# Attention scores in rounded and rest parts, two reordered item pipelines' starts, and a graph-attention shift built from one-column operations, in a one-core four-block kernel

## The reference, cut to what matters

```python
qkv = nodes @ Wqkv.T + bqkv                                    # attention, block 1
q = q.reshape(n, H, DH) * DH ** (-0.5)
scores = jnp.einsum('nhd,mhd->hnm', q, k)
probs = jax.nn.softmax(scores, axis=-1)
attn = jnp.einsum('hnm,mhd->nhd', probs, v).reshape(n, D)
...
gates = jax.nn.softmax(x @ Wg + bg, axis=-1)                   # experts, block 2
topg, topi = jax.lax.top_k(gates, 2)
h = jax.nn.gelu(jnp.einsum('bnc,ech->ebnh', x, W1) + b1, approximate=False)
y = jnp.einsum('ebnh,ehc->bnec', h, W2) + b2
...
e = jax.nn.leaky_relu(a_src[src] + a_dst[dst], NEG_SLOPE)      # graph attention, block 3
m = jax.ops.segment_max(e, dst, num_segments=n)
ex = jnp.exp(e - m[dst])
```

## Time and profile before

| | |
|---|---|
| median of 3 runs | 1318.64 us (1318.53 to 1323.35) |
| the profiled execution's own time | 1322.17 us |
| its span | 1320.1 us |
| busy: PE, PEld, DVE, ACT, POOL | 95%, 84%, 71%, 45%, 8% |
| attention heads | about 500 to 625 us |
| first expert block's items | about 665 to 1003 us |
| graph attention, first layer's heads | about 1079 to 1151 us |

### The profile page before, as it was taken

One profiled execution on the slowest core, in us unless ns is written; L12 is line 12 of the kernel. 1 busy time (PEld: TensorE's weight loads), 2 busy tenths in 40 slices (PEclk: granted clock), 3 DMA queues, 4 the chain that ended last, 5 costly groups with the idle time before them and its releaser, 6 DMA issues. The chain is left out here.

```text
span 1320.1 us, 19406 instructions
## 1 busy us (share of the span) xinstructions
PE 1251.7 (95%) x7067; PEld 1111.7 (84%) x7068; DVE 942.5 (71%) x1771; ACT 598.0 (45%) x1044; POOL 107.0 (8%) x111
## 2 busy tenths in 40 slices
PE   5999999999999999999999999999999888899997
PEld 4777569999999996776999999999998778896864
DVE  6577665583583476668879999999998788736624
ACT  4111143341441245346438888898885227412210
POOL 0000100000000000000030000000002018500111
PEclk9999999999999999999899999999999999999899
DMA  9531190420420610024366999999998210008135
GB/s 348 168 95 33 46 361 24 156 72 1 156 72 1 239 51 0 1 73 155 144 251 242 377 391 392 392 389 394 382 399 278 92 29 1 1 1 298 48 109 166
DMA packets 80704, 225.47 MB, mean 171 GB/s; under 512 B 5185, under 2 KB 17025, under 8 KB 80513
## 3 DMA queue, kind: packets, MB, share of 16 engines
q1 hardware_dynamic: 72736, 187.64, 38.4%
q0 software_dynamic: 7904, 36.97, 7.8%
HBM read 197.85 MB, written 26.74 MB: 170 GB/s over the span
## 5 line engine op out<-in xcount | busy, mean ns | idle before, releaser
L2297 DVE TENSOR_TENSOR part_slot<-slot,item_hi 128x768 fp32r<-128x768 f32 x156 | 138.7, 954 | 1.9 <-ACT item_hi L1673 1.5
L1673 ACT ACTIVATE item_hi<-slot 128x768 fp32r<-128x768 f32 x156 | 118.1, 833 | 30.6 <-DMA slot<-in_e0w 24.8
L2306 DVE TENSOR_TENSOR part_slot<-slot,item_hi 128x768 fp32r<-128x768 f32 x132 | 116.6, 953 | 0.6 <-ACT item_hi L1681 0.2
L1681 ACT ACTIVATE item_hi<-slot 128x768 fp32r<-128x768 f32 x132 | 99.2, 832 | 10.3 <-DMA slot<-in_e0w 10.3
L756 PE MATMUL dve_ps<-item_hi,x_hi 128*128 128x384 f32 x288 | 99.3, 345 | 1.3 <-DVE part_slot L2297 1.0
L756 PE MATMUL act_ps<-item_hi,hid_hi 128*128 128x384 f32 x288 | 99.1, 344 | 0.3 <-DVE hid_lo L2500 0.3
L757 PE MATMUL act_ps<-part_slot,hid_hi 128*128 128x384 f32 x288 | 97.4, 338 | 0.0
L758 PE MATMUL dve_ps<-item_hi,x_lo 128*128 128x384 f32 x288 | 97.2, 338 | 0.0
L758 PE MATMUL act_ps<-item_hi,hid_lo 128*128 128x384 f32 x288 | 96.7, 336 | 0.0
L757 PE MATMUL dve_ps<-part_slot,x_hi 128*128 128x384 f32 x288 | 95.7, 332 | 0.0
L1537 ACT ACTIVATE h_t<-act_ps,par 128x256 f32<-128x256 f32 x36 | 21.1, 585 | 106.9 <-PE act_ps L880 106.9
(11 more groups left out here) (442 smaller groups left out, 3308.2 us busy)
## 6 DMA issues: line engine op xcount, KB each, us to landing
slot<-in_e0w SPq DMA_DIRECT2D x48, 2304.0 KB, 10.5
slot<-in_w SPq DMA_DIRECT2D x9, 2304.0 KB, 8.7
experts<-in_e1w SPq DMA_DIRECT2D x8, 1152.0 KB, 15.7
ea_raw<-in_edge SPq DMA_DIRECT2D x8, 1024.0 KB, 5.6
slot<-in_wqkv SPq DMA_DIRECT2D x3, 2304.0 KB, 15.3
xs<-zrow POOLq DMA_DIRECT2D x2, 3072.0 KB, 15.7
item_x<-xs SPq DMA_DIRECT2D x16, 384.0 KB, 9.5
ys<-item_y POOLq DMA_DIRECT2D x16, 384.0 KB, 6.5
```

Of the source, the lines that this page charges most:

```text
L1673: go(item_hi[j][k][:, :], slot[s][:, k * D:(k + 1) * D], ACT.Copy).then_inc(up_high[j], 1)
L1681: go(item_hi[j][k][:, :], slot[s][:, k * D:(k + 1) * D], ACT.Copy).then_inc(down_high[j], 1)
L2297: vv.tensor_tensor(part_slot[s][:, ks], slot[s][:, ks], item_hi[j][k][:, :].bitcast(F32), ALU.subtract).then_inc(up_low[j], 1)
L2306: vv.tensor_tensor(part_slot[s][:, ks], slot[s][:, ks], item_hi[j][k][:, :].bitcast(F32), ALU.subtract).then_inc(down_low[j], 1)
```

## The change

- The query and the key are split like the other operands. ScalarE rounds the query (`high_query`: two Copies, after VectorE's `query`), and `key` now writes rounded parts. VectorE makes the rests (`low_query`: two subtractions; `low_key`: two `scalar_tensor_tensor` from the bank). The half of the key that the next scores need is made first and has a signal of its own; the bank is freed by the second half's rest. Scores are `mm_parts`.
- The first item's iteration is written out in another order: the down product comes before the next item's up product, its weights are rounded and subtracted while the first up product runs, and SP loads the second item's down weights before the third item's up weights. Some dummy matmuls go.
- In `graph_front` the two 128x4 operations become eight of 128x1 with one SBUF tile input each and a per-partition scalar (one after each masking step, four at the end).
- The load of `slot_iota` is issued later, as its place now holds the query's rounded part before.

```diff
 def scores(i):
-    pe.wait_ge(sig.dve_freed, v0 + HEAD_UNIT[f"q{made_of(i)}"] + 1)
-    pe.wait_ge(sig.act_freed, a0 + HEAD_UNIT[f"k{made_of(i)}"] + 1)
+    pe.wait_ge(qv_low, parted(f"q{made_of(i)}"))
+    if i == made_first(made_of(i)):
+        pe.wait_ge(qv_low, parted(f"k{made_of(i)}"))
+    else:
+        pe.wait_ge(sig.act_freed, a0 + HEAD_UNIT[f"k{made_of(i)}"] + 1)
...
-        mm(bank[:, :], query_of(i)[:, t * P:(t + 1) * P], key_of(i), start=True, stop=True
-           ).then_inc(sig.to_act, 1)
+        mm_parts(bank[:, :], (high[:, ts], low[:, ts]), key_of(i), start=True, stop=True).then_inc(sig.to_act, 1)
...
 # ScalarE
+def high_query(b):
+    act.wait_ge(sig.dve_freed, DVE0["heads"] + HEAD_UNIT[f"q{b}"] + 1)
+    chunk, hd = chunk_of(b)
+    go(q_hi[:, b % 2, :], q_t[:, b % 2, :], ACT.Copy)
+    go(q_split_hi[chunk, hd, :], q_split[chunk, hd, :], ACT.Copy).then_inc(qkv_high, 1)
...
                 for name in BETWEEN[i].split():      # after the exponentials, before prb_hi
                     if name[0] == "k":
                         key(int(name[1]))
+                    else:
+                        high_query(int(name[1]))
 # VectorE
                 divide(i)
...
+                for name in BETWEEN[i].split():      # after low_out, where slot 5 has it; before prb_lo
+                    if name[0] == "k":
+                        low_key(int(name[1]))
+                    else:
+                        query(int(name[1]))
+                        if f"q{made_of(i + 1)}" == name:
+                            low_query(int(name[1]))
...
                 if i + 1 < NH:
                     maxima(i + 1)
+                    for name in BETWEEN[i].split():
+                        if name[0] == "q" and f"q{made_of(i + 1)}" != name:
+                            low_query(int(name[1]))
 # TensorE, items
-iteration(0)
+turn_hidden(0)
+spend(up_banks[0][0], 6)
+pe.wait_ge(x_low, 4)
+for j, s in enumerate(run.down_slots):
+    times_down(0, j, s, down_low, 0)
+times_up(1)
+turn_x(2)
 with pe.Fori(1, last) as k:
 # ScalarE, items
 keep_rows(run, 0); x_in(0)
+high_down(0, 0)
 keep_rows(run, 1)
+high_down(1, 0)
 x_in(1)
-iteration(0, True)
-with act.Fori(1, last) as k:
+gelus(0)
+high_up(0, 1, down_used, 0)
+high_up(1, 1, down_used, 0)
+x_in(2)
+iteration(1, True)       # high_up(0, 2), gelus(1), high_up(1, 2), high_down(0), high_down(1), ...
+with act.Fori(2, last) as k:
 # VectorE, items
-for j in range(2):
-    hidden(0, j)
+hidden(0, 0); low_down(0, 0); hidden(0, 1)
 x_in(1)
+low_hidden(0); low_down(1, 0); low_up(0, 1); result(0); low_up(1, 1)
 share_last(run)
-iteration(0, True)
+hidden(1, 0); hidden(1, 1); x_in(2)
+iteration(1, True)
 # VectorE, graph attention
+    if t:
+        then(raise_max(t - 1))       # tensor_scalar(gdec[..., t], gmax[..., t], a_dst[:, t], 0.0, add, max)
...
-vv.scalar_tensor_tensor(gdec[:, b, 1, :], gmax[:, b, :], -5.0, part_dst[:, 1, :, g % GH], ALU.mult, ALU.subtract)
-vv.scalar_tensor_tensor(gdec[:, b, 2, :], gmax[:, b, :], -1.0, gdec[:, b, 1, :], ALU.mult, ALU.min).then_inc(g_dec, 1)
+raise_max(NT - 1).then_inc(sig.dve_freed, 1)
+for t in range(NT):
+    last = vv.tensor_scalar(gdec[:, b, 2, t:t + 1], gdec[:, b, 1, t:t + 1], -4.0, gmax[:, b, t:t + 1], ALU.mult, ALU.subtract)
```

More of the change, by code:

```diff
@@ L74 @@
 BETWEEN = ("q1 k1", "q2 k2", "q3", "k3 q4", "k4 q5", "k5", "", "")
+HIGH_ORDER, LOW_ORDER = ["v0", "q0", "k0", "k0 second"], ["q0", "k0", "v0"]
+for _i in range(NH):
+    _late = ["v1"] if _i == 0 else []
+    for _name in BETWEEN[_i].split():
+        HIGH_ORDER += [_name] if _name[0] == "q" else [_name, _name + " second"]
+    HIGH_ORDER += _late
+    LOW_ORDER += BETWEEN[_i].split() + _late
 HEAD_UNIT = {"q0": 0, "k0": 0, "score0": 1}
@@ L491, in made_of, with made_first, whole_first, rounded @@
             return hd if hd < WHOLE else 3 * (hd - WHOLE) + 2
+        def made_first(b):
+            return next(i for i in range(NH) if made_of(i) == b)
+        def whole_first(b):
+            return HEADS[made_first(b)] < WHOLE
         def query_of(i):
             hd = HEADS[i]
-            return q_t[:, hd % 2, :] if hd < WHOLE else q_split[:, hd - WHOLE, :]
+            return (q_hi[:, hd % 2, :], q_lo[:, hd % 2, :]) if hd < WHOLE else (
+                q_split_hi[:, hd - WHOLE, :], q_split_lo[:, hd - WHOLE, :])
         def key_of(i):
             hd = HEADS[i]
-            return k_t[:, hd % 2, :] if hd < WHOLE else k_split[:, hd - WHOLE, :]
+            return (k_hi[:, :], k_lo[:, :]) if hd < WHOLE else (k_split_hi[:, hd - WHOLE, :], k_split_lo[hd - WHOLE][:, :])
+        def rounded(name):
+            return HIGH_ORDER.index(name) + 1
+        def parted(name):
+            return LOW_ORDER.index(name) + 1
         def chunk_of(b):
@@ L611, in _ @@
                 up_of(run0, 0, j)
+            sp.wait_ge(sig.to_act, ACT0["heads"] + HEAD_UNIT[f"score{NH - 1}"] + NT)
+            sp.dma_start(slot_iota[:, :], iota_d[0:P].partition_broadcast(P)).then_inc(in_tri, 16)
             sp.wait_ge(sig.to_dve, DVE0["wo"] + 8)
@@ L634, in stream_items @@
                 load_x(2)
-                with sp.Fori(1, last) as i:
+                for j, s in enumerate(run.down_slots):
+                    sp.wait_ge(down_used[j], DC)
+                    down_of(run, first, j, s)
+                second = expert(2)
+                for j in range(2):
+                    sp.wait_ge(up_used[j], 2 * DC)
+                    up_of(run, second, j)
+                sp.wait_ge(x_turned, 6)
+                load_x(3)
+                with sp.Fori(2, last) as i:
                     next_up = expert(i + 1)
@@ L1634, in high_attn @@
                 go(attn_hi[:, k, :], attn_t[:, k, :], ACT.Copy).then_inc(attn_high, 1)
+            high_query(0)
             key(0)
@@ L2239, in _ @@
             query(0)
+            low_query(0)
+            low_key(0)
             maxima(0)
@@ L2533, in stream_items @@
                 low_up(1, 0)
-                for j in range(2):
-                    hidden(0, j)
+                hidden(0, 0)
+                low_down(0, 0)
+                hidden(0, 1)
                 x_in(1)
-                share_last(run)
-                iteration(0, True)
-                with dve.Fori(1, last) as k:
+                low_hidden(0)
+                low_down(1, 0)
+                low_up(0, 1)
+                result(0)
+                low_up(1, 1)
+                share_last(run)
+                hidden(1, 0)
+                hidden(1, 1)
+                x_in(2)
+                iteration(1, True)
+                with dve.Fori(2, last) as k:
                     iteration(k)
```

98 lines of the change are left out of this document (65 added, 33 removed).

## The result

The changed kernel takes 1329.94 us (median of 13 runs, 1325.14 to 1333.39) against 1319.04 for the one before (1313.73 to 1326.89): a ratio of 1.0062 [1.0044, 1.0080], 8.2 us slower by that ratio, which is what everything below is measured against (the two medians alone stand 10.9 apart; the runs of the kernel before spread over 13 us). The profiled execution has a span of 1327.4 us, 7.3 more. The prediction said 1316.8. The time lies above its range, on the other side of no change.

A forecast was written before the change was run, and what follows sets the result against it. It took TensorE to bound the attention, TensorE and VectorE the item stream, VectorE the graph attention. Graph attention -3.9, attention +2.6 and items -0.6 sum to -1.9, on the median 1318.64 about 1316.8 us, range 1312 to 1321.

The forecast's parts named there:

- the first head's "0": Attention, first head: query and key split with nothing before them, +0.7 on the start, -0.7 in the matmuls: 0.
- the start of the third item's up product: Items' start: after the third item's rows are turned at 711.8, its up product starts at 715.2.
- the late rounding: Attention, three slots: ScalarE's queue holds high_query ahead of the probabilities' rounding; scores end +0.93 us later per slot, +2.8.
- the one-column operations: Graph attention: 128x1 operations run beside GpSimd without a stall, 0.07 us each; about 0.75 gained per stalled head.
- The graph attention, -3.9: Graph attention: sum of gains from replacing VectorE's stalled 128x4 operations, -3.9 us, bounds -0.7 and -4.3.
- GpSimd's and ScalarE's loop of 7.2: Graph attention: their own loop per head, about 7.2 us, against 7.1 for the new VectorE loop.
- Rival B: Graph attention: one-column operations take the lock and wait for GpSimd steps, +13 to +25, total 1334 to 1345; chance 0.10.
- The attention, +2.6: Attention: late roundings +2.8, other slots -0.4, slot 5 +0.5, last head -0.35; sum +2.6 us, bounds -5.2 and +4.5.
- The items, -0.6: Items' start: gains of 1.0 and 0.65 against 1.0 lost to the clock; sum -0.6 us, bounds -6 and +2.
- 0.65 more because weights come earlier: Items' start: a gain of 0.65 us from earlier weights, an item taking 27.12 instead of 27.77.
- my term of +1.0: Items' start: TensorE's new idle stretches without dummy matmuls lower the clock, a loss of 0 to 1.7, taken as 1.0.
- Rival C: Whole kernel: splits cost more and stalls cut the clock; attention +4.5, items +2, graph attention -2, total 1323; chance 0.13.

The follow-up runs named there:

- the parts alone: The kernel before with only the attention's, only the items' or only the graph attention's edits, three kernels: +5.9, +2.9 and -2.8 us.
- graph_only: The kernel before with the graph attention's one-column operations alone: ratio 0.9979 to the kernel before, -2.8 us.
- items_only: The kernel before with the items' new order alone, attention and graph attention as before: ratio 1.0022, +2.9 us.
- scores_only: The kernel before with the attention's edits and the move of the index load alone: ratio 1.0045, +5.9 us.
- weights_between: late_rounding with the items' old order and ScalarE's rounding of the next layer's weights between a head's ReLUs and exponentials: ratio 0.9970 to the kernel before.
- first_dummies: late_rounding with the items' old order and 8 dummy matmuls ahead of TensorE's wait for the first head's split key: ratio 0.9965 to the kernel before.
- late_rounding: The changed kernel with ScalarE's query rounding moved behind the probabilities' rounding in slots q3, k3 q4, k4 q5: ratio 1.0017 to the kernel before.
- in company: The items' new order within late_rounding, against late_rounding with the items in their old order (0.9977 to the kernel before): costs 5.3 us.
- split_load: late_rounding with the load of the third item's first half of up weights in two parts, the first issued sooner: ratio 0.9986 to the kernel before.
- fewer_dummies: late_rounding with 4, 5, 11 and 8 dummy matmuls ahead of TensorE's four waits in the second item: ratio 1.0014 to the kernel before.
- up_first: late_rounding with the second half of the third item's up weights rounded and subtracted ahead of the second item's gelus: ratio 1.0018 to the kernel before.

## Why the prediction was wrong

The sum was -1.9; the parts alone measured +6.0 and the whole +8.2. Two steps failed, the first head's "0" and the start of the third item's up product; two terms were mis-sized, the late rounding and the one-column operations.

**The graph attention, -3.9, measured -2.8: mechanism right, size off.** No one-column operation waited for GpSimd. The interval [-4.8, -0.7] holds -3.9 too; the trace is what shows the size. One operation costs 0.12 to 0.13 in the stream (maskings 0.74 apart with one between them, 0.60 without; four in 0.50), not the 0.07 that I took. Per head 1.42 goes, and the wait of 0.13 ahead of it; 0.25, 0.44 and 0.50 come in: -0.35, as the loop's 7.87 to 7.52 says, where I had 0.75, so the five heads give 1.75 and not 3.75. What the rest of the -2.8 is stays open: from the first masking to the second layer's it is 115.36 us before and 113.52 in `graph_only`, but 113.16 in `items_only` and 116.07 in `scores_only`, whose graph attention is unchanged. I held GpSimd's and ScalarE's loop of 7.2 ready as the next bound; `weights_between` shows that VectorE's own is it. Rival B's mechanism is refuted: the longest of 72 took 0.22. The Trainium skill, "SBUF — State Buffer", section "Who interferes with whom", says that `tensor_scalar` can take the lock in a two-port mode, where its operands meet conditions; the prediction took it without them. In this trace none of the 72 at 128x1 waited. (B's upper price was mis-added as well: 7 heads at 4.4 are 31, not 25.)

**The attention, +2.6, measured +5.9: one step failed, one was mis-sized.** What failed is "The first head: query and key are both split with nothing before them, +0.7 on the start, -0.7 in the matmuls: 0". The +0.7 is there: TensorE now waits 2.26 us instead of 1.51. But the lower clock follows for 3.4 us, and the whole is +1.96; `first_dummies` takes 1.57 of it back without a shorter wait and leaves 0.35, so the saving in the matmuls doesn't quite pay for the start either. I had priced the clock in the items and not here. What was mis-sized is "+0.93 per slot": it is 1.57, 1.31 and 1.33, 4.2 for three instead of 2.8. Without the late rounding slots 2 and 3 save 0.65 (`late_rounding`), near the 0.69 worked out, though that came by a misreading: the first values' matmul starts at 552.61 and not 0.23 ahead of 553.25, so the old scores end at 552.61; from the scores' start to the values' second matmul it is 3.68 before and 3.11 in `late_rounding`. The late rounding costs 1.73, 1.96 and 1.96, not 1.62. Slots 0 and 1 saved 0.03 and 0.16 instead of 0.4 together; the distances around slot 5 give +0.24 instead of +0.5; the last head's -0.36 came as said.

**The items, -0.6, measured +2.9 alone and +5.3 in company.** I walked the order to within some 1 us up to the turning of the third item's rows: the first down product starts at 686.41 for 685.4, the rows are turned at 713.02 for 711.8, and of the two waits of 3.4 and 4.2 us there are 2.98 and 2.20, the first behind `gelus(1)` as named. The step that failed is "the third item's up product starts at 715.2": in `items_only` it starts at 718.41. I let the weights be there, "0.65 more because weights come earlier". But SP's load of them waits until the second item's up product has freed their place, and that product now stands behind a down product: 705.70 instead of 694.62. ScalarE gets the weights at 716.5, and the product is 3.2 us late, 1.2 from the walk and 2.0 from this. `split_load` shows it: loaded sooner, the later steps of the second item move by 2.03. The rest of the loss, some 1 to 3 us, is not resolved, and ScalarE's rounding behind `x_in(2)` stands untested; that it isn't the clock (my term of +1.0) `fewer_dummies` shows, and that moving the gelus doesn't help, `up_first`. That it is larger in company than alone is within the intervals.

**The chances.** Slower had 0.13, of which 0.10 stood on rival B, a mechanism that never came. Rival C, "the splits cost more and the stalls cut the clock", is the nearest to what happened, at 0.13 and at 1323; its bounds, +4.5 and +2, were set by single rows, with neither the first head's clock nor the late load in them.

## What to carry to other kernels

An operation that waits for another engine delays all that is queued behind it on its own; place it behind what is already due, here that gave back 5.9 of 8.2 us. When products are reordered, walk the loads as well: each waits for the product that frees its place, and an in-order queue of loads moves with it. Price a new wait of TensorE twice, once for itself and once for the clock behind it, but believe the second price only where TensorE is the bound in that stretch: in the traces dummies gained 1.6 us in the attention's start and nothing among the items, where VectorE and the transfers set the pace.

## What was not expected of the hardware

A dummy of 128 columns of float32 took 0.25 us (twelve instructions for six of them in 1.5 us). A `tensor_scalar` of one column lasts 0.21 us, but costs the stream only 0.12 to 0.13, beside GpSimd's additions too. Of two waits of like length, 2.26 us at 510 and 2.20 us at 744.51 in `items_only`, each was followed by a stretch of 3.41 us at the lower clock; the wait filled with eight dummies down to 0.47 was followed by none. But the length of a wait doesn't settle what follows it: 2.23 us in the same place in `split_load` were followed by twice as long a stretch (0.83 over 505 to 525), and of two waits behind eight dummies, 2.05 us at 713.99 before and 2.04 at 747.77 in `fewer_dummies`, the first was followed by a clock of 0.58 over 714 to 718 and the second by none (1.00 from 690 to 770).
